# A routing step in another sequence on three engines, with the score bias folded into the weights

## The reference, cut to what matters

```python
x = x + attention(layernorm(x), ctx, ctx)      # x: 16 batches x 256 tokens x 256, ctx: 120 tokens a batch
h = layernorm(x)                               # before the experts
logits = h @ Wr.T + br                         # 8 experts
topk_vals, topk_idx = top_k(logits, 2); topk_w = softmax(topk_vals)
out = sum over e: cw_e * (gelu(h @ W1[e].T + b1[e]) @ W2[e].T + b2[e])
x = x + layernorm(out + h) * ln_w + ln_b
```

## Time and profile before

| | us |
|---|---|
| median of 3 runs | 652.23 (650.58 to 652.34) |
| profiled execution, its own time | 648.82 |
| its span, first to last instruction | 646.9 |
| PE / DVE / ACT / POOL busy | 558.2 / 427.6 / 282.9 / 350.5 |
| last transfer of the front issued by POOL | 177.00 |
| first expert matmul on PE | 189.69 |

### The profile page before, as it was taken

One profiled execution on the slowest core, in us unless ns is written; L12 is line 12 of the kernel. 1 busy time (PEld: TensorE's weight loads), 2 busy tenths in 40 slices (PEclk: granted clock), 3 DMA queues, 4 the chain that ended last, 5 costly groups with the idle time before them and its releaser, 6 DMA issues.

```text
span 646.9 us, 17861 instructions
## 1 busy us (share of the span) xinstructions
PE 558.2 (86%) x4922; PEld 497.7 (77%) x4923; DVE 427.6 (66%) x1292; ACT 282.9 (44%) x723; POOL 350.5 (54%) x464
## 2 busy tenths in 40 slices
PE   6999989996578999999999999999999999997000
PEld 5899889885457898989898989898898988775000
DVE  1688888887735576666757575757575766445494
ACT  3687777775334434333333333343434243331142
POOL 4027666677741464656465555565555545542397
PEclk8999999998559999999999999999999999999555
DMA  7756566755432342323232322223232323221753
GB/s 256 245 168 209 185 201 214 214 182 167 144 100 44 37 51 50 49 49 49 49 48 49 47 50 42 55 41 56 41 57 40 56 29 48 43 37 24 226 171 130
DMA packets 64387, 63.92 MB, mean 99 GB/s; under 512 B 15656, under 2 KB 59632, under 8 KB 63952
## 3 DMA queue, kind: packets, MB, share of 16 engines
...
## 4 chain that ended last, share of the span: by engine, by line
PE 66%; POOL 10%; DVE 8%; issue 7%; DMA 7%; ACT 1%; POOLq 1%; DVEq 0%; SPq 0%; ACTq 0%
PE bank L829 11%; PE bank L831 10%; PE bank L830 10%; PE bank L851 10%; PE bank L853 9%; PE bank L852 9%; POOL slot_table L563 6%; DMA slot_table<-rows_now,slots 4%; PE bank L808 2%; DVE w1hi L1303 2%; DVE w2lo L1290 2%; POOL rn L539 1%; DMA z_rows<-xn,sidx 1%; PE bank L747 1%; DVE st L1085 1%
## 5 line engine op out<-in xcount | busy, mean ns | idle before, releaser
L989 ACT ACTIVATE stage<-bank,b1s 128x256 f32<-128x256 f32 (+1 forms) x312 | 125.0, 452 | 178.6 <-PE bank L831 137.7
L598 POOL DMA_INDIRECT z_rows<-xn,sidx x71 | 114.3, 1609 | 145.8 <-DVE xn L1237 120.1
L829 PE MATMUL bank<-xnt,w1hi 128*128 128x256 f16 (+1 forms) x624 | 164.4, 265 | 7.0 <-issue 3.5
L830 PE MATMUL bank<-xnt,w1hi 128*128 128x256 f16 (+1 forms) x624 | 163.7, 264 | 0.0
L831 PE MATMUL bank<-xnt,w1lo 128*128 128x256 f16 (+1 forms) x624 | 163.6, 264 | 0.0
L851 PE MATMUL bank<-w2hi,stage 128*128 x568 | 154.9, 273 | 2.6 <-DVE xn L1237 2.4
L1218 DVE CAST stage<-stage 128x512 f16<-128x512 f32 (+1 forms) x156 | 75.2, 482 | 121.3 <-PE bank L853 121.1
L852 PE MATMUL bank<-w2lo,stage 128*128 x568 | 154.8, 273 | 0.0
L853 PE MATMUL bank<-w2hi,stage 128*128 x568 | 154.8, 273 | 0.0
L1220 DVE TENSOR_TENSOR stage<-stage 128x512 f16<-128x512 f32 (+1 forms) x156 | 102.3, 656 | 5.4
L580 POOL DMA_INDIRECT xn<-tokens_dram,gidx x71 | 73.2, 1032 | 43.9 <-PE bank L808 26.5
...
## 6 DMA issues: line engine op xcount, KB each, us to landing
...
```

Of the source, the lines that this page charges most:

```text
L598: nc.gpsimd.indirect_dma_start(out=z_rows, out_offset=bass.IndirectOffsetOnAxis(ap=sidx[p][:, t:t + 1], axis=0), in_=y_sb[p][:, t, :], in_ ...
L829: nc.tensor.matmul(dst, w1hi[:, col], xhi[:, k, 0:bt], start=(k == 0), stop=False)
L830: nc.tensor.matmul(dst, w1hi[:, col], xlo[:, k, 0:bt], start=False, stop=False)
L989: ins = nc.scalar.activation(h32[:, c * bt:(c + 1) * bt], f_h[q][:, (c % 2) * bt:(c % 2 + 1) * bt], ACT.Gelu, bias=b1s[p][:, c:c + 1], sca ...
```

## The change

The sequence within a step is rewritten on PE, ACT and DVE, and on POOL the copy of the token numbers is put ahead of the norm.

- Score bias: the weights `mt` of the scores are rewritten once in the setup (scaled by 1/16, and a column `lift` added to them), and `xnt` is stored as xn + 1, so that the product carries the bias itself. The 257th column, `s_diag`, its matmul and `ident_c` go. The scale is in `mt`, so the maximum can be negated in the reduction and `neg` alone is left. The setup gets two reductions and three small operations on DVE and two passes over `mt` on ACT.
- Small routing operations: the two subtractions for `leads` become one, `ixf` goes since the comparison reads integers, `slots` is written by the reduction itself, and the wait for `leads` on POOL goes.
- Sequence: see the rows below and the diff.

The diff, cut to the lines that the text speaks of:

```diff
+                if publish is not None:
+                    m, p = publish
+                    b = 2 * m + p
+                    n = TJ * TOPK
+                    at_least(pool, published[p], ROUTED * m)
+                    nc.gpsimd.tensor_copy(rows_now[p][:, :, 0:2], ids[:, bass.ds(b * n, n), :]).then_inc(rows_copied, 1)
...
                 if publish is not None:
                     if isinstance(b, int) and b == 0:
                         pool.wait_ge(table_blank, 16 * PADS)
-                    at_least(pool, published[p], ROUTED * m)
-                    nc.gpsimd.tensor_copy(rows_now[p][:, :, 0:2], ids[:, bass.ds(b * n, n), :]).then_inc(rows_copied, 1)
                     pool.wait_ge(rows_copied, b + 1)
-                    alone(pool, leads_ready, b + 1, tally_pool)
                     alone(pool, slots_ready, b + 1, tally_pool)
...
+                if project is not None:
...
+                    ins.then_inc(ctxt_mm, 1)
+                if route is not None:
+                    mr, pr = route
+                    r = 2 * mr + pr
+                    pe.wait_ge(xn2_ready, r + 1)
+                    pe.wait_ge(xnt_ready, min(t - 1, NB) if isinstance(t, int) else t - 1)
+                    turned(b_x, xn2[pr], x2t_mm)
...
                     for j in range(TJ):
                         for k in range(KD):
-                            nc.tensor.matmul(b_s[:, j, :], xnt[:, k, j * P:(j + 1) * P], kt[:, k, :],
-                                             start=(k == 0), stop=False)
-                        ins = nc.tensor.matmul(b_s[:, j, :], ones[0:SK, :], s_diag[pa], start=False, stop=True)
+                            ins = nc.tensor.matmul(b_s[:, j, :], xnt[:, k, j * P:(j + 1) * P], kt[:, k, :],
+                                                   start=(k == 0), stop=(k == KD - 1))
                     ins.then_inc(s_mm, 1)
...
+                transpose_group(t, project, 1)
                 if project is not None:
-                    pe.wait_ge(xn_ready, b + 1)
-                    at_least(pe, xn2t_ready, b - 2)
-                    turned(b_x, xn[p], xt_mm)
-                if project is not None:
+                    pe.wait_ge(ctxt_ready, b + 1)
+                    at_least(pe, v_ready, b)
+                    for k in range(KD):
+                        ins = nc.tensor.matmul(b_v, ctxt[:, k, :], wvt[:, k, :], start=(k == 0), stop=(k == KD - 1))
+                    ins.then_inc(v_mm, 1)
...
+                    pe.wait_ge(xn_ready, b + 1)
+                    at_least(pe, xn2t_ready, b - 2)
+                    turned(b_x, xn[p], xt_mm)
...
-                nc.scalar.copy(mt[:, c, :], bank[c][:, 0:D])
-                ins = nc.scalar.copy(wv_ext[:, c, 0:D], bank[2 + c][:, 0:D])
+                nc.scalar.activation(mt[:, c, :], bank[c][:, 0:D], ACT.Copy, accum_out=row_sum[:, c:c + 1])
+                ins = nc.scalar.copy(wvt[:, c, :], bank[2 + c][:, 0:D])
             ins.then_inc(setup_ev, 1)
...
-            nc.scalar.copy(wv_ext[:, :, D], bank[5][:, 0:2])
-            nc.scalar.copy(g_col[:, :], bank[5][:, 2:4])
-            nc.scalar.copy(c_col[:, :], bank[5][:, 4:5]).then_inc(setup_ev, 1)
+            nc.scalar.copy(w_bias[:, :], bank[5][:, 0:KD])
+            nc.scalar.mul(c_col[:, :], bank[5][:, 4:5], SCALE / D).then_inc(setup_ev, 1)
             act.wait_ge(setup_ev, 3)
-            nc.scalar.activation(ident_c[:, :], ident[:, :], ACT.Identity, scale=c_col[:, 0:1]).then_inc(setup_ev, 2)
+            act.wait_ge(lift_ready, 1)
+            for c in range(KD):
+                nc.scalar.activation(mt[:, c, :], mt[:, c, :], ACT.Identity, bias=lift[:, c:c + 1], scale=SCALE)
+            nc.scalar.activation(g_col[:, :], bank[5][:, 2:4], ACT.Identity, bias=c_col[:, 0:1], scale=SCALE).then_inc(setup_ev, 2)
...
+                high_part(t, project, 0)
...
-                                                   scale=SCALE, accum_out=psum_p[:, j:j + 1])
+                                                   accum_out=psum_p[:, j:j + 1])
                     ins.then_inc(exp_ready, 1)
-                high_part(t, project, 0)
-                if project is not None:
-                    act.wait_ge(xt_mm, b + 1)
-                    nc.scalar.copy(xnt[:, :, :], b_x).then_inc(xnt_ready, 1)
+                high_part(t, project, 1)
                 if project is not None:
                     act.wait_ge(k_mm, b + 1)
...
+                    act.wait_ge(xt_mm, b + 1)
+                    nc.scalar.activation(xnt[:, :, :], b_x, ACT.Copy, bias=1.0).then_inc(xnt_ready, 1)
                 if attend is not None:
                     act.wait_ge(pt_mm, a + 1)
                     nc.scalar.copy(pt[:, :, :], b_pt).then_inc(pt_ready, 1)
-                high_part(t, project, 1)
-                if measure is not None:
-                    mn, pn = measure
-                    act.wait_ge(rn_ready, t + 1)
-                    at_least(act, xt_mm, t - 1)
-                    normalised(xn[pn], 2 * mn + pn, u, 0, xn_ready)
-                high_part(t, project, 2)
...
+                high_part(t, project, 2)
+                if measure is not None:
+                    mn, pn = measure
+                    act.wait_ge(rn_ready, t + 1)
+                    at_least(act, xt_mm, t - 1)
+                    normalised(xn[pn], 2 * mn + pn, u, 0, xn_ready)
...
-            nc.vector.tensor_copy(bq_rep, bqk[:, 0, :].unsqueeze(2).to_broadcast([P, KD, P])).then_inc(bq_spread, 1)
+            dve.wait_ge(proj_w_loaded, 48)
+            chain(nc.vector.tensor_reduce(bq_net[:, :], wqkv[:, 0, :, :], AX.X, ALU.add))
+            chain(nc.vector.tensor_tensor(bq_net[:, :], bqk[:, 0, :], bq_net[:, :], ALU.subtract))
+            nc.vector.tensor_copy(bq_rep, bq_net[:, :].unsqueeze(2).to_broadcast([P, KD, P])).then_inc(bq_spread, 1)
+            dve.wait_ge(setup_ev, 3)
+            chain(nc.vector.tensor_tensor(lift[:, :], w_bias[:, :], row_sum[:, :], ALU.subtract))
+            nc.vector.tensor_scalar(lift[:, :], lift[:, :], SCALE / D, None, ALU.mult).then_inc(lift_ready, 1)
...
-                    nc.vector.tensor_reduce(top[:, :], b_s, AX.X, ALU.max).then_inc(max_self, 1)
-                if attend is not None:
-                    dve.wait_ge(max_self, 2 * a + 1)
-                    nc.vector.tensor_scalar(neg[:, :], top[:, :], -SCALE, None, ALU.mult).then_inc(max_ready, 1)
+                    nc.vector.tensor_reduce(neg[:, :], b_s, AX.X, ALU.max, negate=True).then_inc(max_ready, 1)
...
-                    dve.wait_ge(slot_self, 5 * k + 4)
-                    nc.vector.tensor_reduce(slotf[:, :], prod[:, :, :, :].rearrange("p j k e -> p (j k) e"), AX.X, ALU.add).then_inc(slot_self, 1)
+                    dve.wait_ge(slot_self, 4 * k + 4)
+                    at_least(dve, published[pk], ROUTED * mk)
+                    with nc.allow_low_precision(reason="a sum of one slot number and zeros"):
+                        nc.vector.tensor_reduce(slots[pk][:, :], prod[:, :, :, :].rearrange("p j k e -> p (j k) e"), AX.X, ALU.add).then_inc(slots_ready, 1)
                 low_part(t, project, 0)
-                if publish is not None:
-                    at_least(dve, published[pk], ROUTED * mk)
-                    dve.wait_ge(slot_self, 5 * k + 5)
-                    nc.vector.tensor_copy(slots[pk][:, :], slotf[:, :]).then_inc(slots_ready, 1)
+                low_part(t, project, 1)
                 if project is not None:
                     dve.wait_ge(v_mm, b + 1)
...
-                    nc.vector.tensor_tensor(v_sb[p], b_v[:, 0:D], bv_bc[0:SK, :], ALU.add)
-                    nc.vector.scalar_tensor_tensor(out=s_diag[p], in0=ident[0:SK, 0:SK], scalar=b_v[:, D:D + 1],
-                                                   in1=ident_c[0:SK, 0:SK], op0=ALU.mult, op1=ALU.add).then_inc(v_ready, 1)
+                    nc.vector.tensor_tensor(v_sb[p], b_v, bv_bc[0:SK, :], ALU.add).then_inc(v_ready, 1)
                 if attend is not None:
                     dve.wait_ge(exp_ready, a + 1)
                     nc.vector.reciprocal(rinv[:, :], psum_p[:, :]).then_inc(max_self, 1)
...
-                low_part(t, project, 1)
                 if route is not None:
-                    alone(dve, top_self, 5 * r + 1, tally_dve)
+                    alone(dve, top_self, 4 * r + 1, tally_dve)
                     for j in range(TJ):
                         ins = nc.vector.max(mx[:, j, :], lg[:, j, :])
                     ins.then_inc(top_self, 1)
+                if route is not None:
+                    alone(dve, top_self, 4 * r + 2, tally_dve)
+                    for j in range(TJ):
+                        ins = nc.vector.max_index(ix[:, j, :], mx[:, j, :], lg[:, j, :])
+                    ins.then_inc(top_self, 1)
+                    at_least(dve, published[pr], ROUTED * mr)
+                    nc.vector.tensor_tensor(leads[pr], mx[:, :, 0:TOPK], mx[:, :, 1::-1], ALU.subtract)
+                if route is not None:
```

(31 more changed lines are left out.)

57 lines of the change are left out of this document (18 added, 39 removed).

## The result

The changed kernel takes 643.79 us (median of 6 runs, 643.07 to 645.13), the kernel before, run beside it, 651.92 (6 runs, 650.14 to 652.34). The ratio is 0.989, 95% interval 0.987 to 0.990: 8.1 us less, where 3.7 were forecast, and outside the stated range of 644.0 to 654.0. The profiled execution took 644.03, its span is 642.3.

What follows compares the result with a forecast made beforehand. The prediction took the two-step ring over the transfers' landing as the bound, the one-step ring taking over. Setup +0.1, ten steps -2.9, last steps -0.9 gave 645.1 profiled, 648.5 as median; own range 646.3 to 650.5, stated 644.0 to 654.0.

Steps and rivals of the forecast that it cites:

- M: End of the statistics operation `mv` on DVE in each step, the number being the step; forecast at 132 us in step 15.
- Long ring: Two-step loop from M over POOL's transfers, their landing and `leads` to M: 17.4 us becomes 15.9, no longer binding.
- the landing: Time from POOL's last transfer issue until DVE can go on; stores begun earlier were to cut 5.5 us to about 4.0.
- rival 1: The landing keeps 5.5 us wherever the burst is: 8.7 a step, 651.3 us; chance 0.25 together with another rival.
- the other end: Gap ahead of POOL's first transfer: 0.28 us if the remaining `alone` runs under `rn`, saving 0.87; 0.84 was taken.
- Short ring: One-step loop M, POOL's norm, third high half, low half, residual, M: 8.20 or 8.76 us, taking over as bound.
- Covers: Slack hiding added work: 0.4 us before DVE needs the scores, 0.45 on DVE before the third low half.
- rival 3: Slower: DVE's routing, packed together, waits for itself; +3.0 us in all, 655.2; chance 0.15.
- Last steps: From step 15 POOL waits for no one; shorter gaps, partly offset by the copy: together 0.9 us less.
- Setup: DVE's first statistics wait for PE's last setup matmuls and ACT's copies: +0.1 us by step 5, from 0 to 2.1.
- From the profiled execution to the median: The profiled kernel before lay 3.4 us below its median; the same difference turned 645.1 into 648.5.
- Rival 4: Better: both covers hold, POOL's remaining `alone` runs under `rn`, idle ahead of `st` goes in six steps: 645.3 us; chance 0.10.

Runs made afterwards that it cites:

- fold_only: The kernel before with only the score bias folded (`mt`, `xnt`, `lift`, no `s_diag`, no `top`): 649.52 us, ratio 0.999 to the kernel before.
- residual_loads_first: The changed kernel with the weights' loads queued ahead of the stores and DVE's residual ahead of its third low part: 640.81 us, ratio 0.985 to the kernel before.
- sequence_only: The changed kernel without the folded bias and without POOL's early copy, leaving the new sequence and merged routing: 652.28 us, ratio 1.003 to the kernel before.
- loads_first: The changed kernel with SP queueing the expert weights' loads ahead of the two `xn2` stores: 641.37 us, ratio 0.986 to the kernel before.
- lift_later: The changed kernel with the third high part ahead of the `xn2` norm and `lift` computed behind the first statistics: 641.73 us, ratio 0.989 to the kernel before.
- loads_first_before: The kernel before with SP queueing the expert weights' loads ahead of the stores, nothing else: 646.01 us, ratio 0.993 to the kernel before.

## Why the prediction was off

- **What bounds.** Right: two rings through M. The long one bound before, and taking its landing away was worth 3.4 us in the kernel before.
- **Long ring: the landing from 5.5 to 4.0.** This step failed; it took 4.7 to 5.4, 5.1 in the mean, and the long ring still binds, as in rival 1. The first store came 1.5 us earlier after M, as worked out (84.58 - 80.92 = 3.66), but the burst, with a hole from 87 to 89 us whose cause is open, lasted 0.6 longer, and the last issue came 0.5 earlier too, so that of the 1.5 only 0.4 was left between issue and burst's end. The ring from M(9) at 80.92 is 6.73 to the last issue, 5.34, and 97.56 - 92.99 = 4.57 to M(11): 16.64, or 8.3 a step.
- **Rival 1's price, 8.7 a step, was 0.4 too high** (6.9 + 5.5 + 5.0 = 17.4 against 16.64). The gap ahead of the first transfer is 0.65 in the loop, between the 0.84 taken and the 0.28 of the other end; and `leads` to M is 4.57 and not 5.0, since `neg` with its waits was worth 0.47 and not 0.27, and the idle times at a round's head are gone. A long operation, 0.87 of residual, now stands ahead of the branch where the 0.17 of `chosen` stood. That this covers the idle is argued, and fits the runs: with `chosen` last, fold_only has 0.42 ahead of `neg` and 0.22 ahead of `st`; with a low half of 0.68 last, residual_loads_first has 0.20 ahead of `st`; with the residual last, the changed kernel has none, while sequence_only, which has `neg` as a second operation, keeps 0.43 ahead of `st`. No run changes that last operation alone.
- **Short ring, 8.20 and 8.76.** It does not bind in the changed kernel. With the landing gone it does, at 8.0 in every step: the mechanism was right, the terms were mis-sized. `neg`, which stands where `top` stood, to M is 97.56 - 95.04 = 2.52 and not 2.85, and the 0.56 more for a round's head does not exist. With 0.56 less in four steps and 0.2 in each (0.33 less there, some 0.15 more ahead of the low half), the forecast of 84.2 becomes 80, the 79.9 of loads_first.
- **Covers.** They held. The routing piece from `mx` to `chosen` takes 93.49 - 91.65 = 1.84, over the 1.5 that the prediction named as a sign of being wrong; but 0.58 of it is the landing, and rival 3 is out. PE does wait for `xn2` (6.3 us in eight steps, and in the kernel before in five steps of eight, not in each), but the scores come in time. Once the landing is gone, the cover is the 0.3 by which the residual's move shortens a step outside a round's head before the scores come last. That `s_diag` and the bias products are worth nothing by themselves is not refuted: `leads` to M in fold_only is 101.53 - 97.69 = 3.84 (4.40 before), and its shorter steps begin there. Two steps share such a piece, so it gives 2.8 of the 3.4; where the rest comes from is not shown.
- **Last steps**, -1.5 for -0.9: the gap is 0.66 to 0.56 where a norm stands ahead, so 0.5 or more a step and not 0.31.
- **Setup**, +1.0 for +0.1, inside the 0 to 2.1 given; lift_later takes 2.1 to 2.5 off M(5) by moving one wait.
- **From the profiled execution to the median.** The other failed step, and the larger one for the number. The difference of 3.4 was carried over from one execution of the kernel before to the median of another kernel. The changed kernel's two profiled executions are 0.2 off their medians, and in the seventeen profiled executions here the difference runs from 3.4 under the median to 0.6 above it, the 3.4 being the largest. 2.6 of it is there at M(5) between the two executions of the kernel before. But a quick setup alone doesn't make it: loads_first_before has one and lies 0.6 above its median. What put this kernel's first profiled execution so far under its median is open.
- **The number.** The forecast was 648.5, the result 643.79, so 4.7 lower. The term from profile to median makes 3.6 of it, and the sum for the profiled execution, 645.1 against 644.03, the other 1.1. In that sum the gains in the ten steps and the last steps were 2.2 and 0.6 too small, and the costs of the setup and of what follows the last issue 0.9 and 0.8 too small, so that errors cancelled. Rival 4, 645.3, came nearest, and only in part for its reasons: the idle ahead of `st` went, the gap on POOL went halfway, and the long ring that it takes as gone still bound.
